# A decoder's TensorE program written out as 24 iterations, and two value products exchanged

## The chip, the core and the metric

One core of one Trainium2 chip runs the whole program. The metric is the device time of one execution in microseconds (us). The kernel before was timed three times: 3147.95, 3152.71 and 3156.04 us, with a median of 3152.71 us. Its five engines are TensorE (PE, with its weight loads shown apart as PEld), VectorE (DVE), ScalarE (ACT), GpSimd (POOL) and SyncE (SP, which issues the DMAs). Each engine has its own instruction stream, and semaphores tie the streams together.

## The reference

Eight sequences of 112 tokens with 256 features pass three cross-attention blocks (the front) and then six decoder layers. The context of each sequence has 375 rows of 128 features. Each decoder layer does this, with 16 heads of 64 features:

```
tn = _ln(t, norm_g, norm_b)
t = _mha(tn, tn, skv, sq, sow, sob, tgt_mask) + t
tn = _ln(t, norm_g, norm_b)
t = _mha(src, tn, ckv, cq, cow, cob, src_mask) + t
tn = _ln(t, pg, pb)
t = t + (jax.nn.relu(tn @ w1 + b1) @ w2 + b2)
```

## The kernel before, in words

The eight sequences are worked on as four pairs (PAIRS = 4, two sequences to a pair). The decoder has L = 6 layers, so there are 24 iterations, one for each layer and pair, and each engine has a loop over the layers with a loop over the pairs inside it. No engine waits at the loop's end for the others: order comes from semaphores that count up over the whole run. What an iteration waits for is a count such as "the proj1 bank has been emptied so many times". The class Place works it out from the iteration's number `it`. In a loop `it` lies in registers; before the loop it is a constant.

The iterations are software-pipelined. Iteration n does, for its own pair, the output product of the self-attention, the cross-attention and the feed-forward. Between these it does the normalisation, keys, queries, scores and sums of the self-attention of the next pair. The last work on TensorE in an iteration is `self_sums(at, 3)` (matmuls at line 769), which multiplies the last probabilities with the values `v`. The head of the next iteration on TensorE, which the change touches, is this:

1. `values(at, (0,))`: the first of four value products. `values` (lines of the helper `project`, matmul at line 581) makes product i for sequence i // 2 and half i % 2 of the features, and puts it into bank proj0 (i even) or proj1 (i odd). A product is two contractions, in four matmul instructions of 512 columns. Its weights are w_kv, and its input is `tnT_next`.
2. `out_rows` with w_o (line 601): the output product, sequence 0 into bank sum1 and sequence 1 into bank proj1.
3. `values(at, (1, 2))`: product 1 (sequence 0, second half, bank proj1), then product 2 (sequence 1, first half, bank proj0).
4. `normed(at, 0, "sum0")`: four transposes (line 573) of the normalised rows, when DVE has signalled `tn_ready`.
5. `values(at, (3,))`, and then the 8 query projections of the cross-attention (c_q, line 581), which need `tnT`, the transposed rows that ACT has copied out.

proj0 is emptied by ACT and proj1 by DVE. In this stretch DVE does, in this order: the mask `cbias` (line 1406); `residual` (line 1398: add the bank sum1, then the bank proj1, to the residual rows `tw`, each followed by statistics); `values(at, 0)` (line 1303: copy product 1 from proj1 into `v`); `normed` (line 1191: the two normalisations, after POOL's `rstd`, line 488; they signal `tn_ready`); `values(at, 1)` (copy product 3 from proj1); the self-attention mask. ACT copies products 0 and 2 from proj0 (line 1039), and then copies out the transposes (line 1020). POOL adds the output bias to the residual rows at line 525 as soon as DVE has finished the rows of the pair before (`t_all`, line 1398).

SP issues all loads, in its own order. Once a layer, in the layer's last pair, it loads the next layer's weights, and there the next self-attention mask (`smask`, line 334) is issued only after SP has waited for the bias addition that follows `tn_ready`. DVE waits for that mask right after `values(at, 1)`.

Of the kernel before, what the change touches and what calls it, by code (L numbers as in the profile page):

```python
# [38 lines left out]
def attention_layers(nc, x, ctx_nat, ctx_tr, self_mask, ctx_mask, front, dec, out):  # L39
# [4 lines left out]

    B, S, E = x.shape
    _, S2, C = ctx_nat.shape
    L, _, HDIM = dec["sa_q"].shape
    P = 128
    EK = E // P
# [5 lines left out]
    PAIRS = B // NB  # L55
# [108 lines left out]
    with scope:  # L164
# [392 lines left out]
        def _(pe):  # L557
# [19 lines left out]
            def project(at, name, weights, moving):  # L577

                bank = fill(at, name)
                for k, (w, m) in enumerate(zip(weights, moving)):  # L580
                    ins = pe.matmul(bank[0:w.shape[1], 0:m.shape[1]], w, m, start=k == 0, stop=k == len(weights) - 1)  # L581
                done(ins, name)

            def out_rows(at, stationary, weights, written=0, slots=("proj1",), between=None):

                counts = dict(at.n)
                for b in range(NB):
                    if between and b == 1:  # L590
                        between()
                    if b < len(slots):
                        bank, col = fill(at, slots[b]), 0
                    else:
                        col = b * E
                    terms = [(a[:, b * S:(b + 1) * S], w) for a, w in zip(stationary, weights)]
                    for k, (a, w) in enumerate(terms):
                        if written and b == 0:
                            name, fills = f"proj{k // written % 2}", len(terms) // 2 // written
                            pe.wait_ge(taken[name], at.emptied(name, counts[name] - fills + k // written // 2 + 1))  # L600
                        ins = pe.matmul(bank[0:S, col:col + E], a, w, start=k == 0, stop=k == len(terms) - 1)  # L601
                    if b >= NB - len(slots):
                        done(ins, slots[b - NB + len(slots)])

            pe.wait_ge(setup_done, 1)
            with pe.Fori(0, ROUNDS) as i:
                at = Place(FRONT_LOOP, i)
# [120 lines left out]
            def values(at, banks_of_values):  # L728

                for i in banks_of_values:  # L730
                    b, n = i // V2, i % V2
                    col = HDIM + n * 512
                    project(at, f"proj{n % 2}", [tnT_next[:, k, b * S:(b + 1) * S] for k in range(EK)],
                            [w_kv[:, k, col:col + 512] for k in range(EK)])
# [39 lines left out]
            at = Place(START)  # L774
# [28 lines left out]

            with pe.Fori(0, L) as l:
                with pe.Fori(0, PAIRS) as p:
                    it = l * PAIRS + p
                    next_layer = (it + 1) // PAIRS
                    at = Place(MAIN_LOOP, it)  # L810

                    def weights(name):
# [7 lines left out]
                        pe.wait_ge(taken[f"sum{i}"], at.emptied(f"sum{i}", 0))  # L820
                    weights("w_o")
                    out_rows(at, [oT[:, c, :] for c in range(HC)], [w_o[:, c, :] for c in range(HC)], slots=OUT_SLOTS)
                    values(at, (1, 2))


                    normed(at, 0, "sum0")
# [729 lines left out]
```

## Time and profile before

| what | us |
|---|---|
| median of three runs | 3152.71 |
| the profiled execution's own time | 3159.5 |
| its span, from the first instruction to the last | 3157.7 |
| PE busy with matmuls | 2910.2 (92%) |
| DVE busy | 1678.7 (53%) |
| ACT busy | 1300.5 (41%) |
| POOL busy | 963.0 (30%) |
| mean granted clock of TensorE | 0.963 of full speed |

The profile shows one execution. The front takes about the first 330 us; after that the 24 iterations follow at about 118 us each. "Issue" is idle time in which an engine waited for nothing that the profile shows. The ends of matmuls are modelled, and neighbouring matmuls overlap in the records: the distance between two starts tells more than a duration.

### The profile page before, as it was taken

To read this page: it belongs to the slowest core of one execution; us is meant where nothing else is said; L and a number is where in the kernel's file an instruction comes from. 1 tells how busy PE (TensorE), PEld (TensorE's weight loads), DVE (VectorE), ACT (ScalarE), POOL (GpSimd) and SP (SyncE) were. 2 spreads that over 40 slices of the span, in tenths; PEclk is the share of its full clock that TensorE was granted. 3 is DMA by queue.
4 is the path that set the end of the run, shared out by engine and by line. 5 is a ranking of instruction groups with operands and counts; after the bars stand their busy time and mean duration, and the time that the engine had idled before them with its cause. 6 is when DMAs were issued, how large, how long until landed. Compare 5 with 4: busy or idle time off the path is not lost.

```text
span 3157.7 us, 72157 instructions
## 1 busy us (share of the span) xinstructions
PE 2910.2 (92%) x23656; PEld 2337.1 (74%) x23656; DVE 1678.7 (53%) x6361; ACT 1300.5 (41%) x4274; POOL 963.0 (30%) x1169
## 2 busy tenths in 40 slices
PE   6675899999999999999999999999999999999999
PEld 4454778778778768778778778778778778777777
DVE  2342546546546546546546546546546546545555
ACT  2222335335335335335335335335344434444444
POOL 0000324324324324324324323323323323323323
PEclk9887899999999999999999999999999999999999
DMA  4002011031111021111022111022111022111010
GB/s 151 26 0 81 1 27 27 2 83 42 55 27 27 2 83 47 50 27 27 2 83 58 39 27 27 2 83 65 32 27 27 2 83 66 31 27 27 2 27 13
DMA packets 132313, 121.56 MB, mean 38 GB/s; under 512 B 15261, under 2 KB 121318, under 8 KB 130278
## 3 DMA queue, kind: packets, MB, share of 16 engines
q1 hardware_dynamic: 131942, 116.53, 14.4%
q8 instruction: 243, 3.98, 0.5%
q14 instruction: 128, 1.05, 0.1%
HBM read 115.59 MB, written 0.92 MB: 37 GB/s over the span
## 4 chain that ended last, share of the span: by engine, by line
issue 51%; POOL 24%; PE 20%; DVE 2%; ACT 1%; POOLq 1%; DMA 0%; SPq 0%; DVEq 0%; ACTq 0%
POOL prob L541 17%; PE proj L581 8%; PE proj L601 3%; POOL prob L511 3%; PE sum L601 3%; PE sum L769 2%; POOL ctx_parts L532 1%; PE proj L573 1%; POOL tw L491 1%; PE score L745 1%; PE tr L756 1%; PE sum L581 1%; DVE qcT L1191 1%; POOLq L540 1%; POOL ctx_parts L529 1%
## 5 line engine op out<-in xcount | busy, mean ns | idle before, releaser
L541 POOL TENSOR_TENSOR prob<-prob,rtotal 128x375 f32<-128x375 f32 x672 | 543.4, 812 | 750.0 <-DVE rtotal L1451 749.0
L961 ACT ACTIVATE prob<-prob,negmax 128x375 f32<-128x375 f32 (+1 forms) x688 | 418.8, 609 | 452.3 <-DVE negmax L1442 421.6
L884 PE MATMUL sum<-pT,ctx 32*128 32x224 f32 (+1 forms) x4608 | 500.6, 358 | 12.6 <-DVE qcT L1434 12.6
L884 PE MATMUL tr<-pT,ctx 32*128 32x224 f32 (+1 forms) x4608 | 500.6, 358 | 0.0
L884 PEld LDWEIGHTS sum<-pT,ctx 32*128 32x128 f32 (+1 forms) x4608 | 417.7, 185 | 73.2 <-issue 53.7
L1442 DVE CUSTOM_DVE_ANT_0 prob<-score,cbias 128x375 f32<-128x375 f32 x672 | 358.3, 533 | 193.5 <-PE score L581 192.1
L884 PEld LDWEIGHTS tr<-pT,ctx 32*128 32x128 f32 (+1 forms) x4608 | 417.0, 185 | 0.0
L581 PE MATMUL score<-ctx_parts,qc_high 128*128 128x376 f32 x1344 | 412.5, 388 | 0.0
L1460 DVE STREAM_TRANSPOSE pT<-prob 128x384 f32<-128x384 f32 x672 | 373.9, 560 | 0.0
L511 POOL TENSOR_TENSOR prob<-prob,rtotal 112x448 f32<-112x448 f32 x200 | 186.4, 932 | 575.8 <-DVE rtotal L1318 575.8
L1032 ACT ACTIVATE prob<-prob,negmax 112x112 f32<-112x112 f32 x800 | 298.9, 377 | 86.3 <-DVE negmax L1336 86.2
L581 PE MATMUL proj<-w_kv,tnT_next 128*112 128x512 f32 x400 | 228.5, 713 | 90.1 <-issue 75.2
L581 PEld LDWEIGHTS score<-ctx_parts,qc_high 128*128 128x128 f32 x1344 | 233.1, 189 | 58.0 <-issue 53.4
L1039 ACT ACTIVATE v<-proj 112x512 f32<-112x512 f32 x50 | 29.9, 597 | 527.9 <-PE proj L581 527.9
L581 PE MATMUL score<-ctx_parts,qc_low 128*128 128x376 f32 x672 | 225.3, 335 | 0.0
L581 PEld LDWEIGHTS proj<-w_kv,tnT_next 128*112 128x112 f32 x400 | 74.7, 203 | 183.5 <-issue 159.6
L581 PE MATMUL proj<-tnT_next,w_q 128*128 128x224 f32 x800 | 188.0, 359 | 0.0
L1336 DVE CUSTOM_DVE_ANT_0 prob<-score,sbias 112x112 f32<-112x112 f32 x800 | 166.9, 270 | 37.0 <-PE score L745 37.0
L581 PE MATMUL proj<-tnT_next,w_kv 128*128 128x224 f32 x800 | 182.7, 352 | 0.0
L486 POOL TENSOR_TENSOR veps<-mv,eps 112x2 f32<-112x2 f32 x78 | 15.3, 196 | 528.9 <-DVE mv L1184 528.9
L581 PE MATMUL proj<-tnT,f 128*128 128x224 f32 x768 | 165.2, 363 | 9.2 <-ACT tnT L1020 9.2
L581 PE MATMUL sum<-tnT,c_q 128*128 128x224 f32 x768 | 164.1, 361 | 5.4 <-DVE oT L1425 5.4
(170 smaller groups left out, 5009.6 us busy)
## 6 DMA issues: line engine op xcount, KB each, us to landing
ctx<-ctx SPq DMA_DIRECT2D x192, 176.0 KB
w_kv<-sa_kv SPq DMA_DIRECT2D x6, 2048.0 KB, 10.0
f<-ff_w SPq DMA_DIRECT2D x12, 1024.0 KB, 9.5
cmask<-ctx_mask SPq DMA_DIRECT2D x24, 375.0 KB, 4.5
w_q<-sa_q SPq DMA_DIRECT2D x6, 1024.0 KB, 11.0
w_o<-sa_ow SPq DMA_DIRECT2D x6, 1024.0 KB, 6.5
c_q<-ca_q SPq DMA_DIRECT2D x6, 1024.0 KB, 7.8
c_o<-ca_ow SPq DMA_DIRECT2D x6, 1024.0 KB, 10.4
```

What stands on the lines that cost most here:

```text
L491: pool.tensor_tensor(tw[:, :, :], tw[:, :, :], bias.unsqueeze(1).broadcast_to([S, NB, E]), ALU.add)\
L511: pool.tensor_tensor(pr, pr, rtotal[0:S, G * g:G * g + G].unsqueeze(2).broadcast_to([S, G, S]), ALU.mult)\
L541: pool.tensor_tensor(row, row, rtotal[:, G * SG + i:G * SG + i + 1].broadcast_to([P, S2]), ALU.mult).then_inc(prob_ready, 1)
L581: ins = pe.matmul(bank[0:w.shape[1], 0:m.shape[1]], w, m, start=k == 0, stop=k == len(weights) - 1)
L601: ins = pe.matmul(bank[0:S, col:col + E], a, w, start=k == 0, stop=k == len(terms) - 1)
L769: ins = pe.matmul(bank[h * D:(h + 1) * D, n * S:(n + 1) * S], v[:, b, col:col + D], probT[0:S, h, duo % 2, n * S:(n + 1) * S], start=True, ...
L884: ins = pe.matmul(bank[:, 0:HT * R], ctx4[keys_of, m // (HALVES // NB), j, :], pT[keys_of, m % 2, :, j * R:(j + 1) * R], start=j == 0, sto ...
L961: act.activation(o, i, ACT.Exp, bias=negmax[0:rows, col:col + 1], scale=scale, accum_out=total[0:rows, col:col + 1]).then_inc(exp_ready, 1)
L1032: ins = act.activation(row, row, ACT.Exp, bias=negmax[0:S, col:col + 1], scale=-1.0, accum_out=total[0:S, col:col + 1])
L1336: ins = dve.tensor_tensor_reduce(out=prob[0:S, k % PROBS, h * S:(h + 1) * S], in0=banks[name][0:S, h * S:(h + 1) * S], in1=sbias[:, g // G ...
L1442: dve.tensor_tensor_reduce(out=prob[:, t % PROBS, 0:S2], in0=banks[name][:, 0:S2], in1=cbias[:, t // TB, :], scale=-SCALE, scalar=3.4e38, ...
L1460: dve.transpose(pT[:, m % 2, i % HT, :], prob[:, i % PROBS, 0:S2B]).then_inc(turned, 1)
```

## The change

Only TensorE's stream is changed. Its two loops over layers and pairs become Python loops, so that the 24 iterations stand one after the other in its program, with constants for every count that it waits for and no branch back. The loops of DVE, ACT, POOL and SP stay, and so does TensorE's loop over the front's rounds. `next_layer` is the same number in another form. And in each iteration product 2 is now issued before product 1.

```
-            with pe.Fori(0, L) as l:
-                with pe.Fori(0, PAIRS) as p:
+            for l in range(L):
+                for p in range(PAIRS):
                     it = l * PAIRS + p
-                    next_layer = (it + 1) // PAIRS
+                    next_layer = l + (p + 1) // PAIRS
                     at = Place(MAIN_LOOP, it)
...
                     out_rows(at, [oT[:, c, :] for c in range(HC)], [w_o[:, c, :] for c in range(HC)], slots=OUT_SLOTS)
-                    values(at, (1, 2))
+                    values(at, (2, 1))
```

## Rows read from the trace of the kernel before

**Rows 1.** Busy time by engine, and cores: span and mean granted clock.
```profile
PE 2910.2 (92%) x23656; PEld 2337.1 (74%) x23656; DVE 1678.7 (53%) x6361; ACT 1300.5 (41%) x4274; POOL 963.0 (30%) x1169
...
core 0: 3157.7 us, clock 0.963
```

**Rows 2.** Waits of PE, 440 to 3040 us: total us, times, longest us.
```profile
PE proj L581 <- issue: 75.2, 23, 3.8
PE sum L884 <- DVE qcT L1434: 11.6, 22, 0.5
PE proj L581 <- DVE tw L1398: 11.4, 22, 0.5
PE proj L573 <- DVE qcT L1191: 6.2, 22, 0.3
```

**Rows 3.** Window of the start: busy us (instructions) of PE, PEld, DVE, ACT, POOL; PEclk; DMA.
```profile
0.00:440.00 440.00, 324.37 (x1921) 243.43 (x1922) 170.65 (x563) 129.13 (x410) 66.67 (x88) 0.87 0.18 51
```

**Rows 4.** Timeline of PE across one loop end: start us, us, line, work, idle before.
```profile
1029.83 0.99 PE L769 MATMUL sum<-pT,v 112*64 112x112 f32 x16
1033.80 3.32 PE L581 MATMUL proj<-w_kv,tnT_next 128*112 128x512 f32 x4 [2.98 <-issue]
...
1040.41 3.62 PE L601 MATMUL proj<-w_o,oT 128*112 128x256 f32 x16
1044.54 3.69 PE L581 MATMUL proj<-w_kv,tnT_next 128*112 128x512 f32 x8 [0.52 <-DVE tw L1398]
1048.07 0.55 PE L573 MATMUL sum<-ident,qcT 112*128 112x112 f32 x4
1048.45 1.88 PE L581 MATMUL proj<-w_kv,tnT_next 128*112 128x512 f32 x4
1050.17 2.06 PE L581 MATMUL sum<-tnT,c_q 128*128 128x224 f32 x10
```

**Rows 5.** Timeline of the same stretch: DVE, POOL and ACT.
```profile
1026.31 0.54 ACT L952 ACTIVATE oT<-sum 128x448 f32<-128x448 f32 x1 [0.45 <-PE sum L769]
1030.68 1.26 POOL L525 TENSOR_TENSOR tw<-t_all,o_bias 112x512 f32<-112x512 f32 x1 [7.38 <-DVE t_all L1398]
1030.87 0.62 DVE L1349 COPY oT<-sum 128x448 f32<-128x448 f32 x1 [0.39 <-PE sum L769]
1033.95 1.05 DVE L1406 TENSOR_SCALAR cbias<-cmask 128x750 f32<-128x750 int32 x1 [2.46 <-issue]
1044.06 0.42 DVE L1398 TENSOR_TENSOR tw<-proj,tw 112x256 f32<-112x256 f32 x1 [2.57 <-PE proj L601]
1045.69 0.70 POOL L488 TENSOR_TENSOR rstd<-veps,minus_half 112x2 f32<-112x2 f32 x1
1046.55 0.69 DVE L1303 COPY v<-proj 112x512 f32<-112x512 f32 x1 [1.21 <-PE proj L581]
1047.16 0.73 DVE L1191 TENSOR_SCALAR qcT<-tw,mv,rstd 112x256 f32<-112x256 f32 x2
```

**Rows 6.** Three gaps on PE elsewhere, and the windows right behind them.
```profile
112.81 0.58 PE L671 MATMUL tr<-ident,prob 112*125 112x112 f32 x3 [1.23 <-ACT pT L952]
115.00:118.40 3.40, 3.40 (x18) 3.40 (x18) 0.28 (x1) 0.53 (x2) 0.00 (x0) 0.50 0.00 0
700.96 1.02 PE L581 MATMUL sum<-tnT,c_q 128*128 128x224 f32 x4 [1.00 <-DVE oT L1425]
701.00:704.40 3.40, 3.40 (x20) 2.75 (x20) 1.25 (x3) 1.32 (x3) 0.00 (x0) 1.00 0.00 0
1172.76 1.55 PE L581 MATMUL sum<-tnT,c_q 128*128 128x224 f32 x4 [2.25 <-DVE oT L1425]
1173.00:1176.40 3.40, 3.40 (x13) 2.21 (x13) 0.39 (x1) 0.27 (x1) 0.00 (x0) 0.52 0.00 0
```

**Rows 7.** DMA queues of instructions: the whole run, then 1031 to 1147 us (packets, MB, share).
```profile
q8 instruction: 243, 3.98, 0.5%
...
q8 instruction: 9, 0.15, 0.5%
```

## The prediction, made before the changed kernel ran

> **What bounds the kernel now.** I read the page first: PE is busy for 92% of the span, the next engine, DVE, for 53% [rows 1]. So TensorE's own stream sets the pace, and the question is where PE is not working. The list of PE's waits between 440 and 3040 us answers it [rows 2]: one row, "issue", holds 75.2 us in 23 times, up to 3.8 us each, and every other row is 0.3 to 0.5 us an iteration. 23 is 24 iterations less one, so I looked at the timeline across one loop end [rows 4]. The last matmul of an iteration belongs to the row at 1029.83 us, which ends at 1030.82, and the first of the next starts at 1033.80, after 2.98 us in which PE waited for nothing that the profile shows. The other engines don't hold it [rows 5]: ACT's last copy ended at 1026.85, DVE's at 1031.49, and the product at 1033.80 (product 0) needs neither of these. The reader is to see there a gap that belongs to PE's own stream: its branch back.
>
> The same rows show a second loss. Product 0's four matmuls last 3.32 us, those of product 3 at 1048.45 only 1.88 us. They are the same instructions, so these run at the lower of TensorE's two levels, 1.2 GHz in place of 2.4, right after the gap. How much that is in all comes from the mean clock: 0.963 over the whole span [rows 1] is a loss of 3157.7 x 0.037 = 117 us of full-speed time, and 0.87 over the first 440 us [rows 3], before any loop end of the decoder, is 57 us of it. About 60 us are left for the decoder.
>
> **The change, part by part.**
>
> *The branch back goes.* 23 gaps, 75.2 us. The front keeps its own loop, the first iteration has no branch before it, and the 24th is followed by nothing. I take all of it. Its bounds: no more than 75.2; not less than what the next work to be late leaves. That is small. Without the gap product 0 starts at about 1030.8 and ends 1.72 us later, at 1032.5. Then `out_rows` needs DVE's copy, done at 1031.49: on time. Its first bank is full some 3.5 us later (two banks in the 1040.41 row's 3.62 us each), at 1036.0. DVE must by then be through its own branch back and the mask, which end at 1033.95 + 1.05 = 1035.0: on time by 1 us, and if it were late, only the second bank, at 1039.5, has somebody waiting behind it. POOL's bias sum ends at 1031.94. ACT has 5 us for its own branch before product 0 is there to be copied. So the loops of the other engines, which stay, lie in cover.
>
> *The half clock goes with it.* About 60 us, of which I leave out what lies inside the gaps themselves or belongs to another gap (the one at 1172.76 us [rows 6] costs 3.4 x 0.48 = 1.6 us), and take 55. The bounds are 50 and 60.
>
> *Constants in place of registers.* TensorE's waits no longer need a count worked out in registers. The rows show no idle time for that between groups of matmuls, apart from the row "issue" already counted, so I take 0. It can only be a gain; above it is bounded by the other rows of the waits, and a tenth of a microsecond at some of them would be a few us in all.
>
> *The products exchanged.* Two things move, and they pull apart.
> First, product 1 goes to bank proj1, which DVE must have emptied of the output product; the wait for that is 0.52 us [rows 4], 11.4 us over 22 iterations [rows 2]. Product 2 goes to proj0, which is long free, so it starts at once, at 1044.54 - 0.52 = 1044.02, and is done at 1045.74 (1.72 us a product: 1048.45 to 1050.17). The wait of 0.52 us is gone. If that were all, the iteration would be 0.5 us shorter.
> But second, DVE's order is fixed: it copies product 1 out of proj1 before it does the normalisation, and the transposes on PE wait for that. Before, the copy started at 1046.55, 2.01 us after product 1 had started at 1044.54, and the second normalisation ended at 1047.89. POOL's `rstd` was ready at 1046.39, before the copy, so the copy is what ends last [rows 5]. Now product 1 starts at 1045.74, the copy at 1047.75, and everything behind it is 1.2 us later: normalisation until 1049.1, transposes at 1049.27 in place of 1048.07. Meanwhile PE has finished product 1 at 1047.46 and stands idle for 1.8 us, with product 3 behind the transposes in its queue and the c_q projections behind ACT's copy of them. All that follows is bound by PE, so the delay is not given back. With the modelled ends the 1.2 may be 1.0; I take 1.1 us an iteration, 24 times: 26 us lost. Queued behind the waiting copy on DVE are the normalisation, product 3's copy and the self-attention mask; SP's load of that mask in the last pair of a layer follows `tn_ready` by a fixed distance and moves along. The ends of this term: a gain of 12 us (0.5 x 24, if DVE's part were covered) and a loss of 29 (1.2 x 24).
>
> *What the new gap does to the clock.* This the trace shows only by neighbours [rows 6]. After a gap of 1.00 us (700.96) the granted clock stayed at 1.00; after one of 2.25 us (1172.76) it was 0.52 for the next 3.4 us; and one of 1.23 us in the front, where PE had smaller gaps beside it, was followed by 0.50. The new gap of 1.8 us lies between. Each time the clock falls costs about 1.6 us (3.4 x 0.48). The ends are none of 24 and all of 24, 0 and 39 us; I take 8 of 24, 13 us, since the surroundings of this gap are densely filled, as at 700.96, but the gap itself is nearer to 2.25.
>
> **Sum**, against the profiled execution's 3159.5 us: 3159.5 - 75 - 55 + 26 + 13 = 3068. The median is 6.8 us below that execution, so by the median it is 3061; I forecast **3060 us**, about 92 less.
>
> Page rules about the branch speak both ways. The Trainium skill's "Advanced Engine Details and Errata", section Control Flow Timing, gives some 51 ns for a branch and 108 ns for one with a comparison; if that were the whole price of a loop end, the removal would be worth about 4 us, and with the exchange the kernel would be slower. The rows have 3.3 us a time, so the price lies elsewhere. "Runtime: NRT & Kernel Launch", section Instruction fetch mechanics, has it: a taken branch out of the loaded pages forces a fetch before execution goes on, while straight code is fetched ahead, its block crossings "mostly hidden". That "mostly" is what the rival C below is about.
>
> **The rivals.**
>
> A. *The exchange pays.* DVE's copy would have to be off the path. For it: the 0.52 us wait is real, and PE gets work into it. Against it: the order in DVE's stream, and a copy that already starts 0.2 us after `rstd` is ready. Then 3152.7 - 75 - 55 - 12 = 3011 us.
>
> B. *The clock falls in every iteration*, because of the gap of 1.8 us that the exchange opens. For it the rows at 112.81 and 1172.76, against it the one at 700.96. 3152.7 - 75 - 55 + 26 + 39 = 3088 us.
>
> C. *Slower: straight code must be fetched too.* The gap at the loop end is at bottom a wait for instructions. The queue that carries them brings 9 blocks in an iteration's 116 us, 243 in the run [rows 7], so the loop's body is fetched anew in every iteration already. No PE wait stands at those other places [rows 2], which says that fetching straight on is hidden. But the program grows to 24 bodies, and if each block then held PE, it decides from 92 / (24 x 9) = 0.43 us a block. At half the price of a loop end (1.6 us a block) it would be 3060 + 24 x 9 x 1.6 = 3406 us. Against it: in the loop the last 8 of 9 blocks are straight code, and DMA traffic beside them doesn't show as waits.
>
> D. *The gap stays.* Another engine's loop end, hidden behind PE's so far, takes its place: DVE idles 2.46 us for its own [rows 5]. It would have to be late by over 1 us more than the working above has it. If half of the gap stayed and the clock still fell, it would be 3152.7 - 38 + 26 = 3141 us, within 0.4% of before.
>
> **How the numbers follow.** The forecast has a chance of 0.70, A 0.10, B 0.13, C 0.04, D 0.03. Within 0.3% (9.5 us, what a measurement of this kernel can tell from no change) only part of D lies. So faster 0.95, same 0.01, slower 0.04. The forecast's own range comes from its terms: exchange 20 to 29, clock 0 to 25, half clock 50 to 60, registers 0 to -10, so 3030 to 3080. The range given reaches to B and most of the way to A: 3025 to 3092.
>
> **What would show each step.** In the changed kernel's profile, PE's "issue" row of 23 times should be gone, and product 0 should start within 0.2 us of the last `self_sums` and last 1.9 us. The time between the starts of two iterations should be about 113 us in place of 118. The wait of PE for DVE's `tw` should be gone, and the transposes at line 573 should wait 1.5 to 1.9 us for DVE in each of the 24 iterations, DVE's copy of `v` just before. The mean clock should rise from 0.963 to 0.97 or 0.98. The prediction is wrong if PE shows "issue" waits inside iterations (C), if the transposes wait no longer than before (A), or if the clock is under 1 once in each iteration (B).

## The result, and the profile after

The changed kernel takes **3049.1 us** (median of four runs, 3047.2 to 3051.2), the kernel before 3152.5 us in the same comparison: a ratio of 0.9676, 95% interval 0.9665 to 0.9688, 103 us less. The forecast was 3060 us in a range of 3025 to 3092.

The page of the changed kernel has PE busy for 94% of a shorter span, and nearly the same busy time on the other engines as in [rows 1]:

```profile
PE 2852.7 (94%) x23656; PEld 2316.1 (76%) x23656; DVE 1679.2 (55%) x6361; ACT 1303.0 (43%) x4274; POOL 963.0 (32%) x1169
...
core 0: 3045.8 us, clock 0.984
```

Its waits of PE between 440 and 3040 us answer to [rows 2]. "Issue" before a value product is gone, and so is the wait for DVE's `tw`. New at the top is the wait of the transposes for DVE, which the exchange brought:

```profile
PE sum L573 <- DVE qcT L1191: 32.9, 23, 1.4
PE sum L884 <- DVE qcT L1434: 12.0, 23, 0.5
...
PE proj L573 <- DVE qcT L1191: 6.5, 23, 0.3
```

The windows answer to [rows 3]: the granted clock between 440 and 3040 us is now 1.00. The first 440 us hold the front, which the change leaves alone: their 0.89 against 0.87 before is a difference between two executions.

```profile
0.00:440.00 440.00, 322.81 (x1947) 242.08 (x1948) 171.24 (x565) 129.12 (x410) 67.62 (x89) 0.89 0.18 51
440.00:3040.00 2600.00, 2529.12 (x21698) 2073.43 (x21699) 1506.91 (x5795) 1173.85 (x3864) 895.39 (x1081) 1.00 0.15 37
```

PE's timeline across the place where the loop ended is the counterpart of [rows 4]. The rows at 1003.41 and 1004.33 touch, where 2.98 us lay idle before, and product 0 lasts 1.97 us in place of 3.32. The row at 1013.04 follows the output product without a wait, and the transposes wait 1.43 us:

```profile
1003.41 0.99 PE L769 MATMUL sum<-pT,v 112*64 112x112 f32 x16
1004.33 1.97 PE L581 MATMUL proj<-w_kv,tnT_next 128*112 128x512 f32 x4
...
1009.59 3.62 PE L601 MATMUL proj<-w_o,oT 128*112 128x256 f32 x16
1013.04 3.60 PE L581 MATMUL proj<-w_kv,tnT_next 128*112 128x512 f32 x8
1018.07 0.60 PE L573 MATMUL sum<-ident,qcT 112*128 112x112 f32 x4 [1.43 <-DVE qcT L1191]
1018.50 1.88 PE L581 MATMUL proj<-w_kv,tnT_next 128*112 128x512 f32 x4
1020.22 3.19 PE L581 MATMUL sum<-tnT,c_q 128*128 128x224 f32 x16
```

DVE and POOL in the same stretch, the counterpart of [rows 5]. POOL's `rstd` ends at 1015.57, but DVE waits for product 1 until 1016.67, copies it, and only then normalises:

```profile
1007.64 0.95 DVE L1406 TENSOR_SCALAR cbias<-cmask 128x750 f32<-128x750 int32 x1 [2.57 <-issue]
...
1014.87 0.70 POOL L488 TENSOR_TENSOR rstd<-veps,minus_half 112x2 f32<-112x2 f32 x1
...
1016.67 0.69 DVE L1303 COPY v<-proj 112x512 f32<-112x512 f32 x1 [2.15 <-PE proj L581]
1017.28 0.72 DVE L1191 TENSOR_SCALAR qcT<-tw,mv,rstd 112x256 f32<-112x256 f32 x2
```

From the start of the second half of the output product to the start of c_q it was 1050.17 - 1040.41 = 9.76 us [rows 4] and is now 1020.22 - 1009.59 = 10.63 us. So the exchange costs 0.87 us an iteration by the timeline, and the loop's removal pays for it several times over.

The queue that carries PE's instructions brings 187 blocks in the whole run in place of 243 [rows 7], though the program is now 24 bodies long:

```profile
q8 instruction: 187, 3.06, 0.4%
```

### The profile page after: what moved, and what is told of

It reads as the page before. It is cut to its first block, busy times and chain, and to the rows that moved or that the text cites. A ratio compares the mean times of both kernels' runs of the same rounds, so it can differ in the third digit from the quotient of the medians.

```text
span 3045.8 us, 69468 instructions
## 1 busy us (share of the span) xinstructions
PE 2852.7 (94%) x23656; PEld 2316.1 (76%) x23656; DVE 1679.2 (55%) x6361; ACT 1303.0 (43%) x4274; POOL 963.0 (32%) x1169
## 3 DMA queue, kind: packets, MB, share of 16 engines
q8 instruction: 187, 3.06, 0.4%
## 4 chain that ended last, share of the span: by engine, by line
issue 49%; POOL 25%; PE 21%; DVE 2%; ACT 1%; POOLq 1%; DMA 0%; SPq 0%; DVEq 0%; ACTq 0%
POOL prob L541 18%; PE proj L581 8%; PE proj L601 3%; POOL prob L511 3%; PE sum L601 3%; PE sum L769 2%; POOL ctx_parts L532 1%; PE proj L573 1%; POOL tw L491 1%; PE score L745 1%; PE tr L756 1%; DVE qcT L1191 1%; PE score L581 1%; POOLq L540 1%; POOL ctx_parts L529 1%
## 5 line engine op out<-in xcount | busy, mean ns | idle before, releaser
L581 PE MATMUL proj<-w_kv,tnT_next 128*112 128x512 f32 x400 | 189.1, 607 | 2.4 <-ACT tnT_next L1020 2.4
L581 PEld LDWEIGHTS sum<-tnT,c_q 128*128 128x128 f32 x768 | 138.8, 190 | 33.0 <-issue 25.1
L581 PEld LDWEIGHTS proj<-tnT,f 128*128 128x128 f32 x768 | 135.7, 190 | 24.9 <-issue 13.7
```

## The experiments

Theory 1 is the prediction's: a loop end costs PE a gap and the half clock behind it, for its branch goes back to instructions that must be fetched anew; and the exchange costs time, because DVE copies product 1 ahead of the normalisation. The rivals: the exchange pays; counts in registers are part of the saving; a taken branch costs 3 us wherever it goes.

### Each half of the change alone

**The straight program in the old order.** Against the changed kernel:

```
-                    values(at, (2, 1))
+                    values(at, (1, 2))
```

> The straight TensorE program with the products in their old order (1, 2). Theory 1 (the exchange costs, because DVE's copy of product 1 ends last before the normalisation): PE waits 0.68 us for proj1 again, but the transposes start 0.8 us earlier after the output product, so 24 x 0.85 = 20 us less than the changed kernel, about 3029 us. Rival (the exchange gains by filling the wait for proj1): 24 x 0.5 = 12 us more than the changed kernel, about 3061 us.

Measured: 3031.8 us (the kernel before, timed beside it, 3150.9; ratio 0.9618, interval 0.9605 to 0.9631). That is 17 us less than the changed kernel.

**The exchange alone.** Against the kernel before:

```
-                    values(at, (1, 2))
+                    values(at, (2, 1))
```

> The exchange alone, TensorE's loops kept. Theory 1: 24 x 0.85 = 20 us more than before, about 3173 us, and more still if the gap of 1.4 us comes on top of a low clock right after the loop end. Rival (the exchange gains 0.5 us an iteration): 3141 us. If the two parts of the change add up without touching each other, this difference to before is the same as that between the changed kernel and the straight one in the old order.

Measured: 3166.5 us (before 3150.9; ratio 1.0048, interval 1.0034 to 1.0062), 15.6 us more. The waits of PE in it, over the whole run, show both things side by side, the loop ends and the new wait:

```profile
PE proj L581 <- issue: 75.1, 23, 3.9
PE sum L573 <- DVE qcT L1191: 34.3, 24, 1.4
```

So the halves add up: -119 us for writing the loop out, +16 to +17 us for the exchange, with and without the loop. The rival by which the exchange pays has fallen. It cost a little less than the 20 us expected. The traces show a reason in each pair. Once in the straight kernel of the old order the self-attention mask came late enough for a gap of 2.20 us, which the changed kernel has at 0.85 us, and behind it the clock fell:

```profile
1133.05 1.82 PE L581 MATMUL sum<-tnT,c_q 128*128 128x224 f32 x4 [2.20 <-DVE oT L1425]
...
1130.00:1137.00 7.00, 4.80 (x19) 3.23 (x18) 1.06 (x3) 0.66 (x2) 0.00 (x0) 0.76 0.04 10
```

That is 1.35 us of gap and 7 x 0.24 = 1.7 us of clock, 3 us in all.

In the pair with loops it is the clock behind the loop ends. In the profiled execution of the kernel before the granted clock fell around all 23 of them, in that of the exchange alone around 18. At the other five it stayed up after a gap of the same length, and product 0 ran at full speed:

```profile
1032.23 1.94 PE L581 MATMUL proj<-w_kv,tnT_next 128*112 128x512 f32 x4 [2.98 <-issue]
...
1032.00:1040.00 8.00, 7.77 (x32) 5.74 (x33) 1.73 (x3) 0.60 (x1) 1.03 (x1) 1.00 0.01 3
```

The mean clocks of the five timed runs say the same, 0.968 to 0.973 against 0.965 to 0.968 before. Why the exchange does this isn't shown. So each pair holds an offset of its own to the 24 x 0.87 = 21 us of the timeline, and that the two differences agree within 2 us is in part chance.

### What the transposes wait for

**DVE normalises first.** Against the changed kernel, in DVE's stream:

```
                     residual(tw)
-                    values(at, 0)
                     normed(at, tw)
+                    values(at, 0)
                     values(at, 1)
```

> The changed kernel with DVE's two steps exchanged as well: the normalisation before the copy of product 1. Theory 1: rstd is ready 2.5 us after the output product, before the value products end at 3.45 us, so the transposes start right behind these, and product 3 waits some 0.5 us for proj1 in place of the 1.4 us gap; c_q starts about 1 us earlier an iteration: 3049 - 25 = 3024 us. If the copy is not what the transposes wait for, nothing changes: 3049 us.

Measured: 3022.9 us (ratio 0.9595, interval 0.9582 to 0.9608), 26 us less than the changed kernel. Moving DVE's copy alone takes the whole wait away: so the copy was what ended last. (No run has this order on DVE together with the old order of the products, so whether the exchange adds to this gain isn't shown.) The timeline shows the transposes right behind the value products, and a short wait for the bank that the copy now frees later:

```profile
1009.06 3.60 PE L581 MATMUL proj<-w_kv,tnT_next 128*112 128x512 f32 x8
1012.49 0.55 PE L573 MATMUL sum<-ident,qcT 112*128 112x112 f32 x4
1013.44 1.97 PE L581 MATMUL proj<-w_kv,tnT_next 128*112 128x512 f32 x4 [0.40 <-DVE v L1303]
```

### Branches, registers and the distance of a jump

**The loop over the layers back, the pairs written out** (5 branches back):

```
-            for l in range(L):
+            with pe.Fori(0, L) as l:
                 for p in range(PAIRS):
```

> The changed kernel with TensorE's loop over the layers back and the pairs within it written out: 5 branches back in place of none, and all waits of the decoder again against registers. Theory 1 (what the straight program saves is the price of branches back, idle and half clock behind it, 119 / 23 = 5.2 us each, the ones between layers some 0.5 us dearer): 3049 + 5 x 5.7 = 3078 us. Rival (part of the saving is the counts in registers, which all waits of the body need again here): at a third of the 119 us, 3049 + 26 + 40 = 3115 us or more.

Measured: 3077.2 us (before 3151.8; ratio 0.9764, interval 0.9749 to 0.9779).

**The loop over the pairs back, the layers written out** (18 branches back):

```
             for l in range(L):
-                for p in range(PAIRS):
+                with pe.Fori(0, PAIRS) as p:
                     it = l * PAIRS + p
-                    next_layer = l + (p + 1) // PAIRS
+                    next_layer = (it + 1) // PAIRS
```

> The changed kernel with TensorE's loop over the pairs back and the layers written out: 18 branches back. Theory 1: 3049 + 18 x 5.0 = 3139 us. Rival (counts in registers cost): the same 3139 as long as the branches take most of it, but then the run with 5 branches lies far above the line between 0 and 18.

Measured: 3137.6 us (ratio 0.9951, interval 0.9936 to 0.9966). PE's "issue" rows of these two, first 5 and then 18 branches, between 440 and 3045 us:

```profile
PE proj L581 <- issue: 15.1, 5, 3.4
```

```profile
PE proj L581 <- issue: 56.9, 18, 3.5
```

With none, 5, 18 and 23 branches back and the same order of products the kernel takes 3049, 3077, 3138 and 3167 us: 5.6, 4.9 and 5.1 us a branch against none. In the run with 5 nearly every wait of the decoder is against a register again, and it lies 3 us above a line of 5 us a branch, where a third of the saving for registers would have put it 40 us above. So the saving goes with the branches, and what registers cost is at most a few us. Two more readings leave less than that. The five branches between layers cost 28.1 us against no branch, with registers coming back beside them, and 28.9 us on top of the other 18 (3166.5 against 3137.6), where registers stand on both sides. And the trace of the run with 5 accounts for its 28 us without them: 15.1 us of "issue"; 4.0 us more of waiting for DVE's copy at line 1425, which is late when the mask is (7.8 us in place of 3.8); and the granted clock at half for six stretches of 3.4 us, 6 x 1.7 = 10 us.

**A near branch at the same place:**

```
-                    pe.wait_ge(taken["proj0"], at.emptied("proj0", 0))
+                    with pe.Fori(0, 2) as i:
+                        pe.wait_ge(taken["proj0"], at.emptied("proj0", 0))
```

> The changed kernel with a loop of two rounds around the first wait of each iteration on TensorE (a wait that is already met): the same count of loop ends at the same place, but each branch back goes to the instruction just before it. Theory 1 (the 3.3 us of a loop end are the wait for instructions from far back, which must be fetched anew): a near branch costs its register work and itself, 0.1 to 0.4 us and in part beside the matmuls still queued, so 3049 to 3058 us. Rival (a taken branch costs PE 3 us wherever it goes): an 'issue' row of 72 us or more and the half clock again, 3049 + 24 x 5 = 3169 us.

Measured: 3048.9 us (before 3152.3; ratio 0.9672, interval 0.9651 to 0.9693): nothing lost that can be measured. No "issue" row before a value product came back between 440 and 3040 us, and the instruction queue brings the same 187 blocks. The first iteration is the one place where PE has no matmuls queued when it comes to the small loop, and there the loop shows: product 0 starts 1.87 us after PE's last matmul, in place of 1.15 in the changed kernel (second line):

```profile
326.19 3.72 PE L581 MATMUL proj<-w_kv,tnT_next 128*112 128x512 f32 x4 [1.87 <-ACT tnT_next L1021]
323.92 3.73 PE L581 MATMUL proj<-w_kv,tnT_next 128*112 128x512 f32 x4 [1.15 <-ACT tnT_next L1020]
```

So two rounds of a near loop take some 0.7 us, with their register work, and in the other iterations they lie beside queued matmuls. A branch back over an iteration stands in the same place and leaves PE idle for about 3 us all the same. So it is not the branch that costs but how far back it goes. That what a far one waits for is the fetch is the nearest reading (the far loops raise the number of blocks, to 207 with 5 branches, 233 with 18 and 243 with 23; how much of that is register instructions isn't shown), but no run varied the distance between one instruction and a whole iteration. The Trainium skill speaks of both halves: "Advanced Engine Details and Errata", section Control Flow Timing, has 108 ns for a branch with a comparison, which the near loop doesn't contradict, though its 0.7 us for two rounds hold register work too and measure no single branch; "Runtime: NRT & Kernel Launch", section Instruction fetch mechanics, has the stall of a branch whose target is no longer loaded, and the far one agrees with that, at 2.85 to 3.9 us in the traces with loops.

### The other engines' loops

**All decoder loops written out**, those of POOL, ACT and DVE too (one of three alike):

```
-            with dve.Fori(0, L) as l:
-                with dve.Fori(0, PAIRS) as p:
+            for l in range(L):
+                for p in range(PAIRS):
```

> The changed kernel with the decoder loops of DVE, ACT and POOL written out too (SyncE keeps its loop). My theory: their branches back lie in cover (DVE's idle of 2.6 us at cbias has nobody waiting), so no change within 3 us of 3049, with DVE's 60 us of issue waits before cbias gone. Rival (one of them takes the place of PE's loop end in part): 10 to 25 us less. A second rival: more instruction fetching by four engines at once shows as waits and costs time.

Measured: 3047.3 us (before 3150.9; ratio 0.9673, interval 0.9660 to 0.9686), the same as the changed kernel. DVE's 60 us of "issue" before the mask are gone from its trace and nobody had waited for them. The same stall on an engine in cover is worth nothing.

### When a gap brings the half clock

**A longer gap**: one more pass of DVE between the copy of product 1 and the normalisation (the counts of `cbias_written` are doubled to fit).

```
                     values(at, 0)
+                    dve.tensor_scalar(cbias[:, :, :], cbias[:, :, :], 1.0, None, ALU.mult).then_inc(cbias_written, 1)
+                    gate(cbias_written, 2 * it + 2)
                     normed(at, tw)
```

> The changed kernel with one more pass of DVE over cbias (times 1.0, about 1.0 us) between the copy of product 1 and the normalisation, so that PE's gap before the transposes grows from 1.4 to about 2.4 us. If a gap of this length still leaves the clock up: 3049 + 24 x 1.0 = 3073 us, mean clock 0.98. If it brings the half clock, as the gap of 2.25 us at 1172.76 us of the kernel before did, each iteration pays some 1.6 us more: 3049 + 24 x 2.6 = 3112 us, and the mean clock falls to about 0.97.

Measured: 3090.3 us (3083.0 to 3095.3; before 3151.8; ratio 0.9796, interval 0.9781 to 0.9811). The pass was cheaper than expected, 0.54 us and 0.23 of waiting, so the gap grew to 2.21 us only. That accounts for 24 x 0.78 = 19 of 41 us. The other 22 are the clock: its mean is 0.975, and one of the iterations where it fell looks so:

```profile
801.95 0.60 PE L573 MATMUL sum<-ident,qcT 112*128 112x112 f32 x4 [2.21 <-DVE qcT L1191]
802.39 2.83 PE L581 MATMUL proj<-w_kv,tnT_next 128*112 128x512 f32 x4
...
803.00:806.40 3.40, 3.40 (x7) 1.93 (x7) 0.87 (x2) 0.56 (x2) 0.24 (x1) 0.53 0.00 0
```

At 1.6 us (3.4 x 0.47) a time, 22 us are 14 falls, and 14 is what the granted clock of the decoder shows: 13 right behind the new gap, and one, at 1153 us, behind a late mask (2.07 us of waiting). So the gap of 2.21 us, the same in all 24 iterations, was followed by the half clock in 13 of them and not in the other 11: neither none nor all, so both figures expected were missed, and the truth is between. What decides between the 13 and the 11 isn't shown. In the same surroundings a gap of 1.43 us never brought it.

### A version that beats both

**Product 3 into bank proj0**, copied by ACT, on top of the kernel with the normalisation first:

```
-                    values(at, (3,))
+                    values(at, (3,), (0, 1, 0, 0))
...
                     normed(at, tnT, norm, "sum0")
+                    chunk(at, v[:, 1, 512:1024], 512)
...
                     normed(at, tw)
                     values(at, 0)
-                    values(at, 1)
```

The tuple names the bank of each product; the constants for the products in each bank change from 2 and 2 to 3 and 1.

> The kernel with the normalisation first (3023 us), and product 3 put into bank proj0 and copied by ACT after tnT, so that it needn't wait for DVE's copy of product 1 out of proj1. Theory 1: the 0.40 us wait before product 3 goes, with some 0.1 of pipeline, 24 x 0.45 = 11 us less: 3012 us. Rival (ACT's extra copy of 0.6 us makes the c_q copies late, or tnT, 0.96 us, is what c_q then waits for): 3023 us or a little more.

Measured: **3010.4 us** (3008.6 to 3013.0; before 3151.8; ratio 0.9550, interval 0.9537 to 0.9563), 39 us less than the changed kernel. All of the stretch is closed up now:

```profile
1002.88 3.62 PE L602 MATMUL proj<-w_o,oT 128*112 128x256 f32 x16
1006.34 3.60 PE L582 MATMUL proj<-w_kv,tnT_next 128*112 128x512 f32 x8
1009.77 0.55 PE L574 MATMUL sum<-ident,qcT 112*128 112x112 f32 x4
1010.15 1.88 PE L582 MATMUL proj<-w_kv,tnT_next 128*112 128x512 f32 x4
1011.87 3.19 PE L582 MATMUL sum<-tnT,c_q 128*128 128x224 f32 x16
```

From the output product's second half to c_q it is 8.99 us, against 10.63 in the changed kernel: 24 x 1.64 = 39 us.

## Why the prediction was right, and where its sizes were off

*The branch back.* Predicted 75 us, all of it. The row with 23 waits is gone entire, and nothing took its place at the loop's end: product 0 starts at once, and DVE's first residual addition waits 1.20 us for PE, not the other way round (the working had 1 us to spare). One reading was loose: not every other row of PE's waits was 0.3 to 0.5 us an iteration. The wait for DVE's copy behind the mask (line 1425), once a layer, was 5.4 us in 5 times, up to 2.2 us; with the change it is 3.8. Rival D (the gap stays) is out, and the run with all loops written out shows that the cover was real.

*The half clock.* Predicted 55 us, worked out from an execution with a mean clock of 0.963; the timed runs beside the experiments had 0.964 to 0.969. Between medians the straight kernel in the old order is 119 us faster than the kernel before. With 75 us for the gaps that leaves 44 for the clock. Between the spans of the profiled executions it is 3157.7 - 3030.0 = 127.7 us, but some of that lies in the front, which nothing changed. The first iteration's product 0 starts there (the kernel before, then the straight one in the old order):

```profile
328.12 3.73 PE L581 MATMUL proj<-w_kv,tnT_next 128*112 128x512 f32 x4 [1.31 <-ACT tnT_next L1020]
325.46 3.72 PE L581 MATMUL proj<-w_kv,tnT_next 128*112 128x512 f32 x4 [1.15 <-ACT tnT_next L1020]
```

From there on the difference is 125 us, so the clock was worth 50 us even in the execution that I summed from, and the term was 5 us too large. The last step of the sum, "the median is 6.8 us below that execution", was right in part only. In all ten other profiles this product starts between 322.67 and 326.57 us, at 325.2 on the mean, so about 3 of the 6.8 us were the front's and rightly taken off. The other 4 or so were half clock in the decoder, by the mean clocks above, and the half-clock term had taken those off already. Together the two made the forecast 9 us too fast.

*Constants in place of registers.* Predicted 0; the run with 5 branches bounds it at a few us, and its trace leaves nothing for it.

*The exchange.* Predicted +26 us, measured +17 and +16. The mechanism is the one predicted, step by step (DVE's copy ends last, the transposes wait, c_q starts later), and its sign too, but the working put the gap at 1.8 us and the loss at 1.2, taken as 1.1 an iteration, where the trace has 1.43 and 0.87. Half of the error is in where product 2 would start: I took the wait's 0.52 us off the old start, though PE's idle time is counted from a modelled end. From start to start it was 4.13 us (1040.41 to 1044.54), and is now 3.45 us, so the wait was worth 0.68 us. The rest is in distances that I carried over: DVE's copy starts 1.91 us after product 1, not 2.01, and the transposes 1.40 us after the copy, not 1.52. Rival A is out.

*The clock behind the new gap.* Predicted 13 us for 8 of 24 iterations; measured none, mean clock 1.00 over the decoder. Rival B is out at 1.43 us. At 2.21 us it would have held in 13 of 24 iterations. No run has the 1.8 us of my working, so whether 8 of 24 fits that gap isn't shown.

*The straight program's own fetching* (rival C): no wait of PE for nothing inside an iteration beyond the 0.2 us rows at line 769 that the kernel before has as well, and fewer blocks than before. Out.

From 3159.5 the corrected sum is 3159.5 - 75 - 50 + 17 + 0 - 3 = 3048.5, against 3049.1. Two terms made the forecast 22 us too slow (the exchange by 9, the clock behind its gap by 13), and two made it 9 us too fast (the half clock by 5, the step to the median by 4). That it came within 11 us owes something to luck: the errors pulled against each other.

## What to carry to other kernels

On the engine that sets the pace, a loop whose body is long costs at each branch back: here 3.3 us of standing still and nearly 2 more at half clock, while a near branch behind queued work and the same loops on the other engines cost nothing that the time shows. Before two products are exchanged to fill a wait, read the order of whoever consumes them: here the consumer took the later one first, and what paid in the end was to move the consumer's copy. And when a sum starts from one execution, ask what its distance from the median is made of: the part that the change removes anyway must not be taken off twice.

## What the runs showed of the hardware

- 24 near loops of two rounds on TensorE cost nothing that could be measured behind queued matmuls (3048.9 against 3049.1 us), and some 0.7 us the one time that nothing was queued. A branch over a whole iteration left PE idle for 2.85 to 3.9 us.
- After a gap of 1.43 us in an otherwise full stretch the granted clock stayed at 1.00 in all 24 iterations. After one of 2.21 us it fell in 13 of 24 (to a mean of 0.53 over the 3.4 us from 803.00). Around the loop ends, with about 3 us idle, it fell 23 times of 23 in the kernel before and 18 of 23 with the exchange alone.
- The straight program of 24 bodies needed 187 instruction blocks (3.06 MB), the looped one 243 (3.98 MB), and the straight one shows no wait of PE for them between 440 and 3040 us.
